# Two slots of 256 rows at the head of an expert stage made one of 512, with its side work moved to other places

## The reference, cut to what matters

```python
x = x + attn(layernorm(x))      # rmsnorm, then q, kv, a = h @ w_qkva.T; a = sigmoid(a)
                                # y[t] = a[t] * y[t-1] + kv[t] along the sequence; attn = q * y
z = layernorm(x)
logits = z @ router_w.T         # 7 routed experts, each row takes the best two
combine = softmax(top 2)
mixed = sum over experts of combine[e] * (silu(z @ w_gate[e]) * (z @ w_up[e])) @ w_down[e]
shared = (silu(z @ sw_gate) * (z @ sw_up)) @ sw_down
x = x + mixed + shared
```

## Time and profile before

| | |
|---|---|
| median of 3 runs | 989.99 us (989.73 to 990.22) |
| profiled execution, its own time | 989.97 us |
| its span, first to last instruction | 988.2 us |
| PE busy | 974.3 us, 99% |
| DVE, ACT, POOL busy | 587.8, 477.6, 395.9 us |
| attention part and its last projection end | 103.96 us |
| slots 0 and 1 on PE | 103.96 to 147.19 us |
| first quad (units 2 and 3) on PE | 147.19 to 180.35 us |

### The profile page before, as it was taken

How to read it: one execution, slowest core, us unless ns; L and a number is a source line. 1 busy time by engine, 2 the same in 40 slices (tenths; PEclk the granted TensorE clock), 3 DMA queues, 4 the chain that set the end, 5 groups by cost and what they waited for, 6 DMA issues and landing times.

```text
span 988.2 us, 15868 instructions
## 1 busy us (share of the span) xinstructions
PE 974.3 (99%) x5565; PEld 849.3 (86%) x5565; DVE 587.8 (59%) x1035; ACT 477.6 (48%) x762; POOL 395.9 (40%) x265
## 2 busy tenths in 40 slices
PE   8999999999999999999999999999999999999997
PEld 6788998888889998888888888888888999999886
DVE  7987787787663234455446544654465455656576
ACT  4555434223322324455545544554455556667563
POOL 3326200000021243365546564655455488776200
PEclk9999999999999999999999999999999999999999
DMA  9333310000039995634563456345534576774393
GB/s 320 104 93 83 87 31 22 11 12 22 1 114 348 322 324 177 197 101 157 178 199 105 157 175 202 81 177 178 200 87 166 188 264 221 275 216 159 120 297 106
DMA packets 146018, 155.06 MB, mean 157 GB/s; under 512 B 75433, under 2 KB 134322, under 8 KB 138802
## 3 DMA queue, kind: packets, MB, share of 16 engines
q1 hardware_dynamic: 139232, 136.08, 42.5%
q0 software_dynamic: 6720, 18.36, 5.8%
q10 hardware_dynamic: 18, 0.01, 0.0%
HBM read 127.67 MB, written 26.74 MB: 156 GB/s over the span
## 4 chain that ended last, share of the span: by engine, by line
PE 89%; DVE 7%; ACT 2%; issue 1%; POOL 0%; DVEq 0%; POOLq 0%; ACTq 0%
PE ps L1147 39%; PE ps L1125 15%; PE ps L1103 11%; PE ps L1128 8%; PE ps L1189 4%; PE ps L1009 4%; PE ps L1169 4%; PE ps L1197 2%; DVE y_sb L1337 2%; PE ps L991 1%; DVE hT_lo L1295 1%; PE ps L1020 1%; ACT h_hi L875 1%; DVE h_lo L1743 1%; DVE ps L1737 1%
## 5 line engine op out<-in xcount | busy, mean ns | idle before, releaser
L1147 PE MATMUL ps<-xs_hi,w_both 128*128 128x512 f32 x1216 | 380.1, 390 | 0.1
L1147 PEld LDWEIGHTS ps<-xs_hi,w_both 128*128 128x128 f32 x1216 | 228.3, 188 | 48.6 <-DVE ps L1737 0.7
L641 POOL TENSOR_TENSOR w_both<-w_raw,w_both 128x2048 fp32r<-128x2048 f32 x45 | 223.2, 4960 | 105.5 <-ACT w_both L812 96.9
L1147 PE MATMUL ps<-xs_lo,w_both 128*128 128x512 f32 x608 | 236.7, 389 | 0.0
L1125 PE MATMUL ps<-w_both,h_hi 128*128 128x512 f32 x656 | 233.0, 398 | 0.1
L1128 PE MATMUL ps<-w_both,h_lo 128*128 128x256 f32 x656 | 184.1, 281 | 0.0
L1743 DVE TENSOR_TENSOR h_lo<-ps,h_hi 128x512 fp32r<-128x512 f32 x152 | 105.1, 692 | 102.8 <-ACT h_hi L875 81.4
L1737 DVE TENSOR_TENSOR ps<-ps,silu 128x512 f32<-128x512 f32 x152 | 106.2, 699 | 93.9 <-ACT silu L868 64.9
L665 POOL DMA_INDIRECT x_stage<-z_rows,idx_x x70 | 73.1, 1044 | 221.5 <-DVE idx_x L1656 160.9
L868 ACT ACTIVATE silu<-ps 128x512 f32<-128x512 f32 x152 | 90.8, 597 | 135.8 <-PE ps L1147 135.6
L1125 PEld LDWEIGHTS ps<-w_both,h_hi 128*128 128x128 f32 x656 | 123.3, 188 | 30.2 <-DVE h_lo L1743 0.4
(11 more groups left out here) (226 smaller groups left out, 1078.3 us busy)
## 6 DMA issues: line engine op xcount, KB each, us to landing
w_raw<-in_L_ffn_w_gate_dram SPq DMA_DIRECT2D x20, 1024.0 KB, 4.9
w_raw<-in_L_ffn_w_up_dram SPq DMA_DIRECT2D x20, 1024.0 KB, 7.2
w_raw<-in_L_ffn_w_down_dram SPq DMA_DIRECT2D x20, 1024.0 KB, 6.0
sorted_rows<-x_stage SPq DMA_DIRECT2D x32, 256.0 KB, 2.2
x_rows<-sorted_rows SPq DMA_DIRECT2D x128, 64.0 KB, 2.0
w_spare<-in_L_ffn_w_up_dram SPq DMA_DIRECT2D x6, 1024.0 KB, 6.2
w_spare<-in_L_ffn_w_gate_dram SPq DMA_DIRECT2D x6, 1024.0 KB, 9.5
w_spare<-in_L_ffn_w_down_dram SPq DMA_DIRECT2D x6, 1024.0 KB, 12.3
```

What stands on the lines that cost most here:

```text
L641: pool.tensor_tensor(w_lo[buf][:, k, :], w_raw[buf][:, k, :], w_hi[buf][:, k, :].bitcast(F32), ALU.subtract).then_inc(wlo_ready[k], 1)
L1147: last = pe.matmul(ps[:, 2 * (j % 2) + part, :], w[:, part, kd * H + j * P:kd * H + (j + 1) * P], xx[:, h // 2, kd, :], start=i == 0, stop ...
```

## The change: what it does

Slots 0 and 1 become `quad(0, ...)` on PE, ACT and DVE. For that both units' rows are turned and split before it: unit 0 in group 6, unit 1 in group 7 (before: unit 0 in group 7, unit 1 within slot 0). Unit 2's rows are turned behind tile 1 of the quad and unit 3's behind tile 4, as in the other quads (before: behind pairs 0 and 2 of slot 1). The last `turn_back` stands ahead of the first tile, the last z is turned into banks 4 and 5, `ranks` stands between the two row tiles of the second half of the down part, and the ranking steps on DVE are spread anew over quads 0 and 2. SP's and POOL's programs are unchanged.

```diff
@@ ACT
-                act.activation(zT[NC - 1][:, :, :], ps[:, 0:2, :], ACT.Copy).then_inc(zT_ready, 1)
+                act.activation(zT[NC - 1][:, :, :], ps[:, 4:6, :], ACT.Copy).then_inc(zT_ready, 1)
...
                     h_rows(g + 2)
+                else:
+                    x_hi(g - (NC - 2), g - (NC - 2))
                 if g + 1 < NC:
                     h_hi_part(g + 1)
-                else:
-                    x_hi(0, 0)
...
-            slot(0, 0, early=True, turns=((2, 1),), between={1: lambda: z_rows(NC - 1), 2: zT_copy})
-            slot(1, 1, early=True, turns=((1, 1), (3, 2)))
+            quad(0, 0, early=True, between={1: lambda: z_rows(NC - 1), 5: zT_copy})
@@ PE
                 pe.wait_ge(z_ready, NC)
-                pe.wait_ge(gated, 5)
+                pe.wait_ge(res_ready, NC)
...
                     pe.wait_ge(res_ready, g)
+                if g == NC - 2:
+                    pe.wait_ge(x_split, 1)
...
+                    if t == ST and JH + 1 in between:
+                        between[JH + 1]()
...
-            slot(0, 0, 0, between={0: last_back, 2: lambda: last_routes(NC - 3),
-                                   6: lambda: last_routes(NC - 2), JH - 1: turn_last_z},
-                 down=lambda: last_routes(NC - 1), skip=0)
-            slot(1, 1, 0, between={1: ranks}, skip=0)
+            quad(0, 0, 0, skip=0, wide=False, between={
+                0: last_back, 2: lambda: last_routes(NC - 3), 4: lambda: last_routes(NC - 2), 5: turn_last_z,
+                7: lambda: last_routes(NC - 1), JH + 1: ranks})
@@ DVE
-                if g == NC - 1:
-                    turn_x(0, LD)
-                scan(g, None if g + 1 < NC else lambda: x_lo(1, 0))
+                if g >= NC - 2:
+                    n = g - (NC - 2)
+                    turn_x(n, LD)
+                    scan(g, lambda: x_lo(n + 1, n))
+                else:
+                    scan(g)
...
-            slot(0, 0, turns=((1, 1, loads(1)),), shared=0, early=True, skip=0, between={
-                ("gated", 0): lambda: statistics2(NC - 1), 1: logits_and_z,
-                2: lambda: take_logits(NC - 2, 7), "down": choices})
-            slot(1, 1, turns=((0, 1, loads(2)), (2, 2, loads(3))), shared=1, early=True, skip=0, between={
-                0: rank_totals, 1: rank_blocks, 2: rank_quarters, "down": kinds_and_places})
+            def totals_and_blocks():
+                rank_totals()
+                rank_blocks()
+                rank_quarters()
...
+            quad(0, 0, turns=ahead_of(0), shared=0, early=True, skip=0, between={
+                ("gated", 0): lambda: statistics2(NC - 1), 2: logits_and_z, 5: lambda: take_logits(NC - 2, 7),
+                "down": choices, "half": totals_and_blocks})
             betweens = {
-                2: {0: pair_targets, 3: lone_places, 6: lone_targets, 7: find_pairs, "down": move_all,
+                2: {0: rank_kinds, 2: places, 3: pair_targets, 5: lone_places, 6: lone_targets, 7: find_pairs,
+                    "down": move_all,
```

More of the change, by code:

```diff
@@ L981, in turn_last_z @@
                         z = z_all[:, (NC - 1) * CT + k, :].rearrange("p (i k) -> p k i", k=KD)
-                        last = pe.transpose(ps[:, kd, k * P:(k + 1) * P], z[:, kd], ident[:, :])
+                        last = pe.transpose(ps[:, 4 + kd, k * P:(k + 1) * P], z[:, kd], ident[:, :])
                 last.then_inc(zT_psum, 1)
@@ L1787, in quad @@
                     gate(n, j, par, early, skip, ps[:, 2 * par + 1, :].rearrange("p (j n) -> p j n", j=2))
+                    if ("gated", j) in between:
+                        between["gated", j]()
                     rest(n, j, par, early, skip, h_lo[:, j, :].rearrange("p (j n) -> p j n", j=2),
@@ L1840, in logits_and_z @@
                 turn_z(NC - 2)
-            def kinds_and_places():
-                rank_kinds()
-                places()
             def move_all():
```

## The result

The changed kernel takes 1009.29 us (median of 6 runs, 1008.24 to 1010.47) against 990.04 for the kernel before in the same comparison: ratio 1.0193, interval 1.0180 to 1.0207. Its profiled execution took 1008.86 us with a span of 1007.1, so the shift to account for is 1007.1 - 988.2 = +18.9 us. The forecast was 1004.6 (+14.65), the range 1000.0 to 1008.0. The sign was right, and the time lies 1.3 us above the range.

The account below looks back on a forecast made before the run. PE, busy for 99% of the span, was taken to bound the kernel. The terms summed to +14.65 us on the profiled 989.97, giving 1004.6 us, with a range of 1000.0 to 1008.0.

Parts of the forecast that it names:

- matmul work, ranks, slot 1's wait: Quad 0 on PE: wide matmuls save 1.2 us net, `ranks` waits +0.2, slot 1's small wait before its down matmuls goes, -0.2.
- unit 0 in group 6, last `turn_back` in front: `x_lo` inside scan 6 delays group 7's low part, +0.6 us; PE's wait for `times_q` is no longer covered, +1.45.
- unit 2's rows: Quad 0: DVE's turn waits for rows loaded behind the last z's store; PE stands ahead of `route(6)`, +8.5 us.
- clock: Behind PE's 8.5 us stand in quad 0, the clock falls to 1.2 GHz before PE resumes, +1.8 us, bounds 0 and 3.5.
- copy of the last z: Quad 0: ACT copies it behind tile 5's rounding and unit 3's `x_hi`, so PE waits at `route(7)`, +1.0 us.
- quad 2: `rank_kinds` and `places` on DVE make tiles 5 and 6 and the last down pairs wait for it, +2.5 us.
- beyond: After quad 2, PE and DVE release the work themselves, so the shift goes unchanged to the end, 0.
- a longer fall: Rival: `route(6)`'s 16 tiny matmuls may not bring the clock back, twice the price, 1006.4 us; chance 0.13.
- the rival in which the rows come in time: Unit 2's load doesn't hold DVE at tile 1; PE waits 1.6 us, no clock fall, 996 us; chance 0.08.
- not slower: Rival: rows come in time and DVE is never late on quad 2 or the copy, 990.6 us; chance 0.02.

Follow-up runs that it names:

- e7: Kernel before, with only the last `turn_back` put ahead of slot 0's first tile: 991.77 us, ratio 1.0020.
- e8: Kernel before, with only `rank_kinds` and `places` moved from slot 1 into quad 2: 992.49 us, ratio 1.0024.
- e11: Kernel before, with `route(5)` issued twice, so 32 matmuls of 7 columns follow each other: 993.08 us, ratio 1.0032.
- e12: Kernel before, with only unit 0 turned and split in group 6 instead of group 7: 990.27 us, ratio 1.0003.
- e1: Changed kernel, with the loads of units 2 and 3 ahead of SP's store of the last z: 1001.5 us, ratio 1.0113.
- e5: Changed kernel, with 36 extra wide matmuls, results unused, ahead of PE's wait for gate 2: 1006.2 us, ratio 1.0166.
- e4: Changed kernel, with extra unused wide matmuls: 36 ahead of `route(6)`, behind the wait for gate 2, and four ahead of `route(7)`: 1012.45 us.
- e9: e6 with `pair_targets`, `lone_places` and `places` re-spaced in quad 2, `lone_targets` and `find_pairs` behind its last gate: 988.96 us, ratio 0.9990.
- e6: Changed kernel with e1's loads, and last `turn_back`, last z's turn, `route(6)`, unit 0's `x_lo` and `rank_kinds` moved: 991.3 us, ratio 1.0011.
- e10: e9 with each route in quad 0 split into two halves of 8 matmuls, six wide ones between: 989.02 us, ratio 0.9987.

## Why the prediction was right or wrong

By its own steps, read from the trace of after:

| step | predicted | measured | read from |
|---|---|---|---|
| matmul work, ranks, slot 1's wait | -1.2 | -1.1 | what the next four rows leave of the shift at quad 2's start, 163.85 - 147.19 = 16.66 |
| unit 0 in group 6, last `turn_back` in front | +0.6 + 1.45 | +2.2 | tile 0 at 107.47; in the earlier trace rows the 12 covering matmuls (1.44) leave 105.27 |
| unit 2's rows | +8.5 | +9.1 | 120.08 to 129.45, less 0.23 |
| clock | +1.8 | +5.3 | `route(6)` +1.7, tile 4 +1.9, tile 7 +1.7 |
| copy of the last z | +1.0 | +1.1 | 143.80 to 145.15, less 0.23 |
| quad 2 | +2.5 | +2.7 | 35.85 - 33.16 |
| beyond | 0 | -0.4 | the next quad starts 19.35 later, the end comes 18.9 later |
| sum | +14.65 | +18.9 | |

The first row is what the others leave and is no measurement of its own. The last one lies at one place. PE's rows of after stay 19.4 us behind those of before until this wait of before, which after doesn't have (it passes from 813.77 to 813.89):

```profile
794.86 0.38 PE L1103 MATMUL ps<-xs_hi,w_both 128*128 128x256 f32 x1 [0.19 <-DVE w_both L1698]
```

From there on the shift is 18.9. The profiled executions of e7, e8, e11 and e12, all variants of the kernel before, don't have that wait either, so it is rather chance than the change.

**Unit 2's rows** were right in mechanism and within 0.6 us. PE resumed 0.95 us later than forecast and came to the stand 0.3 later. The delay is POOL's `bias`, 0.54 us where the earlier trace rows have 0.23, a landing some 0.3 later than reckoned, gate 0 0.1 later, and 0.26 us from the end of `turn_z(6)` (127.90 + 1.29) to the first tiny matmul, for which the forecast had nothing. e1 shows that SP's order is the cause, so the rival in which the rows come in time falls.

**Quad 2** was right in all three places, by the price of each as read above: +1.3, +0.5 and +0.64 against +1.4, +0.5 and +0.6. e8 shows it alone.

**The step that failed is the price of the clock.** I took the nearest row, 14 transposes after an idle start, for 1.8 us, and gave a longer fall 0.13 and 1006.4. That row is the excess over its own 3.25 us and says nothing of how long the clock stays low when other work opens the restart. The prediction did name the reason, that `route(6)`'s sixteen tiny matmuls may not bring the clock back, and then did not follow it. From the resumption at 129.45 it stayed low for 7.5 us: 3.4 of the route and 4.1 of tile 4. At half rate the loss is half of that, 3.7, and e5 measured 3.4. The right way was to take the burst and a tile of wide work behind it at half rate: 1.7 for the route and up to 2.8 for the tile, 4.5 at most. The other 1.7 us, the second fall, were missing altogether: I priced the wait for the copy at its length and did not ask what a wait and sixteen tiny matmuls do to the clock. So the mechanism of the first fall was right and its size was not, while the second fall lay outside the mechanism forecast. With the two falls at their measured sizes (3.6 and 1.7 in place of 1.8), the prediction's sum is 18.15, or 1008.1. (Its rival "not slower" leaves the +0.2 of the ranks out of the sum: 990.8 in place of 990.6, which changes nothing.)

The Trainium skill (TensorE: Matmul & The Clock Gate, Part 1) tells of a kernel in which PE idles only briefly between groups of matmuls and its clock swings between the two levels nevertheless. The rows of after, e4 and e9 agree: the fall behind `route(7)` came with waits of 0.96, 0.27 and 0.28 us ahead of it. Had I weighed that beside the page's plainer rule on long idling, which I went by, the second fall would have been a rival.

What stays open: why the clock falls behind `route(7)` in some executions and not in others with the same wait (0.28 us with a fall in e9's trace, 0.27 without one in e6's), and whether tiny matmuls alone, without a wait, do it (e11 did not settle it). e10 shows a remedy, in eleven executions, and not the rule.

## What to carry to other kernels

A DMA wait that is moved forward on an in-order engine takes all behind it along: when a consumer (here DVE's turn of unit 2) moves, its load must move on its own queue as well, and that one edit was worth 7.8 us. Price a stand of PE with what it runs next: if that is a burst of tiny matmuls, reckon up to half rate for the burst and for most of the wide tile behind it, and look at every shorter wait that stands ahead of such a burst; with the burst split among wide matmuls, none of e10's eleven executions was of the slower group. Where each tile leaves a side engine 0.7 us to spare, two pieces of 1.8 and 1.6 us between its gates cost 2.3 us (e8); with `rank_kinds` in the quad before and two other pieces behind the last gate there was no wait (e9).

## What the runs showed of the hardware

- The clock fell to 1.2 GHz after a stand of 2.16 us that sixteen matmuls of 7 columns followed (e1), and behind a wait of 0.27 us, four wide matmuls and such a burst (e4). It did not fall in the traces in which 1.94 us of standing were followed by eight matmuls of 128 columns and wide or narrow ones (after and e7, at 106), nor behind the bursts that had no wait ahead of them (after, 113.02 to 114.72; e11, 32 in 3.5 us), nor in one of two traces with 0.27 or 0.28 us ahead of the burst (e6; e9 had the fall). In after, where nothing ran, the fall was read 3 us into the stand of 9.
- Sixteen matmuls of 7 columns took 3.4 us at the low clock and did not end it (after, 129.45 to 132.86); it was back at 137.0, within tile 4.
- Such a route takes 1.7 us at 2.4 GHz, 0.107 each, nearly as much as a matmul of 256 columns (0.12).
- A wait that the timeline gives as 0.20 us cost 0.47 (after, 182.11): gaps between issues tell the price, not the idle time recorded.
